# A closing mixture of experts computed in 71 row blocks of each token's two experts, with the decay stage's table products on VectorE

## The reference

```python
# decay attention: phases and decays by position, per head
qph = q * phase_prog;  kph = k * phase_prog_inv
inner = (einsum(qph, kph) * mask) @ v;  cross = (q * phazor_prog * phazor) @ last_conv
t = t + (inner + cross).real
# closing mixture, hidden width 192, top 2 of 8
z = layer_norm(t)
vals, idx = top_k(z @ Wg + bg, 2);  gates = softmax(vals)
h = gelu(einsum('bne,xeh->bnxh', z, W1) + b1)
expert_out = einsum('bnxh,xhe->bnxe', h, W2) + b2
out = t + sum_k gates[k] * expert_out[idx[k]]
```

## Time and profile before

| | us |
|---|---|
| median of three runs | 4375.7 |
| span of the profiled execution | 4435.5 |
| first mixture, blocks (window 2256 to 2630) | 374 |
| decay stage, from its first DMA at 2629.4 to 3681.6 | 1052 |
| closing mixture, from 3681.6 to the end | 754 |

### The profile page before, as it was taken

The page is one execution under the profiler, slowest core; times in us unless marked ns, Lnnn a source line. Parts: engine busy times, 40 slices in busy tenths (PEclk is TensorE's granted clock), DMA queues, the critical chain, the costliest instruction groups (busy, mean ns, idle before and its releaser), DMA issues. The chain is left out here.

```text
span 4435.5 us, 74474 instructions
## 1 busy us (share of the span) xinstructions
PE 3699.2 (83%) x21807; PEld 1993.2 (45%) x21809; DVE 3136.1 (71%) x6481; ACT 2174.3 (49%) x3800; POOL 1933.4 (44%) x2119
## 2 busy tenths in 40 slices
PE   2479999999999999999569962888888886999999
PEld 0212333333333333332258851555555555777777
DVE  7478888888887878887156646555555557877777
ACT  3326666666666666666357740222222223444443
POOL 1111333233223333332345552666666644777776
PEclk9679999999999999999789985999999998999999
DMA  2121111122222222220033320000000001000000
GB/s 97 20 37 28 31 30 30 30 38 38 36 37 38 38 39 38 38 37 11 18 117 103 103 78 10 25 29 28 26 28 28 27 16 34 24 24 24 24 20 23
DMA packets 98451, 166.17 MB, mean 37 GB/s; under 512 B 27904, under 2 KB 33288, under 8 KB 98072
## 3 DMA queue, kind: packets, MB, share of 16 engines
q1 hardware_dynamic: 81208, 129.14, 12.2%
q0 software_dynamic: 16384, 33.59, 2.7%
q10 hardware_dynamic: 576, 0.02, 0.0%
HBM read 89.70 MB, written 72.97 MB: 37 GB/s over the span
## 5 line engine op out<-in xcount | busy, mean ns | idle before, releaser
L1214 ACT ACTIVATE b_probs<-b_ps_s 128x512 f32<-128x512 f32 x2048 | 1174.4, 596 | 673.0 <-PE b_ps_s L1258 609.9
L1016 DVE TENSOR_REDUCE b_maxes<-b_ps_m 128x1 f32<-128x1024 f32 x1024 | 1218.2, 1216 | 312.9 <-PE b_ps_m L1246 288.4
L1258 PE MATMUL b_ps_s<-b_qs,b_ks 99*128 99x512 bf16 x2048 | 790.6, 390 | 83.8 <-DMA b_qs<-b_m_parts 23.4
L1246 PE MATMUL b_ps_m<-b_ks,b_qs 96*128 96x512 bf16 x2048 | 638.5, 394 | 64.2 <-DVE b_maxes L1016 43.5
L1985 POOL TENSOR_TENSOR e_act_lo<-e_act,e_act_hi 128x512 fp32r<-128x512 f32 x384 | 522.6, 1361 | 238.9 <-DVE e_act_hi L1914 238.9
L1258 PEld LDWEIGHTS b_ps_s<-b_qs,b_ks 99*128 99x128 bf16 x2048 | 198.7, 98 | 882.5 <-ACT b_probs L1214 668.2
L1270 PE MATMUL b_ps_o<-b_probs,b_vs 128*32 128x512 f32 x4096 | 551.8, 611 | 23.6 <-ACT b_probs L1214 22.8
L2186 ACT ACTIVATE e_act<-e_ps_h,e_bias 128x512 f32<-128x512 f32 x384 | 264.4, 689 | 411.3 <-PE e_ps_h L2240 290.6
L935 POOL DMA_INDIRECT slots_in<-b_xn,b_slot x256 | 251.6, 983 | 413.2 <-ACT b_probs L1214 367.0
L2089 DVE TENSOR_TENSOR e_act<-e_act,e_ps_g 128x512 f32<-128x512 f32 x384 | 261.6, 682 | 145.7 <-ACT e_act L2186 145.7
L2777 DVE TENSOR_TENSOR d_inner<-d_ps_s,d_decay 128x512 f32<-128x512 f32 x256 | 169.3, 682 | 221.6 <-PE d_ps_s L3059 109.3
(11 more groups left out here) (462 smaller groups left out, 7089.7 us busy)
## 6 DMA issues: line engine op xcount, KB each, us to landing
b_qs<-b_q_parts SPq DMA_DIRECT2D x96, 256.0 KB
c_xin<-slots_in SPq DMA_DIRECT2D x71, 256.0 KB, 2.6
slots_out<-c_y_out SPq DMA_DIRECT2D x71, 256.0 KB, 2.0
b_q_parts<-b_qparts SPq DMA_DIRECT2D x16, 768.0 KB
a_x<-in_x_dram SPq DMA_DIRECT2D x8, 1024.0 KB, 10.2
normalised_t<-d_xT SPq DMA_DIRECT2D x16, 512.0 KB
e_xb<-normalised_t SPq DMA_DIRECT2D x32, 256.0 KB, 2.8
out_dram<-e_total SPq DMA_DIRECT2D x32, 256.0 KB, 2.0
```

The lines of the kernel that those rows point to most:

```text
L1016: nc.vector.tensor_reduce(maxes[:, kv, u:u + 1], ps_m[:, u % 2], AX.X, ALU.max).then_inc(m_free, 1)
L1214: nc.scalar.activation(probs[:, s % PROBS, j * HALF:(j + 1) * HALF], ps_s[:, j % 2], ACT.Exp).then_inc(exp_done, 1)
L1246: last = nc.tensor.matmul(ps_m[:, u % 2, half * HALF:(half + 1) * HALF], qs[0:STACK, buffer, h * PX + qt * P:h * PX + qt * P + P], ks[0:ST ...
L1258: nc.tensor.matmul(ps_s[:, j % 2], ks[0:rows, parity, kv * PX + tt * P:kv * PX + tt * P + P], qs[0:rows, parity, h * PX + half * HALF:h * ...
```

## The change

In the decay stage three things change. The products with the tables move from GpSimd to VectorE, which reads `d_ps_q` in PSUM and adds the bias in the same instruction; ScalarE's copy `d_raw` is gone. For each of a token's two experts a "card" of 130 numbers is laid (the normalised token, its gate weight, its own pair number), a rank among the tokens of the same expert is computed by 9 small matmuls with a triangle of ones, and GpSimd scatters the cards (16 indirect DMAs an image) into `cards_in`. The transposed tokens are no longer stored to DRAM, and the loop over images has two images in its body.

`mixture_stage` is replaced by `cards_stage`, 71 blocks of 512 cards of one expert each (hidden width 192 as 128 + 64), whose result rows are weighed and scattered by GpSimd to the pair's own row in `pair_rows` (4 indirect DMAs a block), and by `closing_stage`, which loads both rows of each token, adds them to the tokens, turns them and writes the output.

```diff
@@ cards_stage: SyncE @@
+            for e in range(E):
+                sp.dma_start(slot_rows(E * REGION + e * SLOTS), xin[:, e]).then_inc(spared, 16)
+            sp.wait_ge(plan, 1)
+            sp.wait_ge(pads_made, 2)
+            for e in range(E):
+                at = sp.value_load(base_i[0:1, e:e + 1], min_val=0, max_val=SLOT_ROWS - SLOTS)
+                sp.dma_start(slot_rows(at), xin[:, e]).then_inc(padded, 16)
+            for e in range(RING_L, E):
+                load_weights(e)
...
+            for j in range(MAX_BLOCKS):
+                load_x(j)
@@ cards_stage: GpSimd @@
+            for j in range(MAX_BLOCKS):
+                pool.wait_ge(x_in[j % RING_X], 16 * (j // RING_X + 1))
+                pool.wait_ge(y_copied, j + 1)
+                for t in range(BT):
+                    nc.gpsimd.indirect_dma_start(
+                        out=pair_rows,
...
+                        in_=y_out[:, j % RING_Y, t], in_offset=None).then_inc(y_sent[j % RING_Y], 16)
@@ cards_stage: VectorE @@
+            for j in range(MAX_BLOCKS):
+                if j + 2 < MAX_BLOCKS:
+                    fetch(j + 2)
+                if j >= 2:
+                    weigh_y(j - 2)
+                if j + 1 < MAX_BLOCKS:
+                    split_x(j + 1)
+                low(j, 0)
+                low(j, 1)
@@ cards_stage: ScalarE @@
+            for j in range(MAX_BLOCKS):
+                first(j, 0)
+                if j >= 1:
+                    add_bias(j - 1)
+                high(j, 0)
+                first(j, 1)
+                if j + 1 < MAX_BLOCKS:
+                    high_x(j + 1)
+                high(j, 1)
@@ cards_stage: TensorE @@
+            for j in range(MAX_BLOCKS):
+                unit(j, 0)
+                if j >= 1:
+                    second(j - 1, 0)
+                    second(j - 1, 1)
+                unit(j, 1)
+                if j + 1 < MAX_BLOCKS:
+                    turn_x(j + 1)
+                if j >= 2:
+                    turn_y(j - 2)
@@ closing_stage: SyncE, VectorE @@
+                for k in range(2):
+                    sp.dma_start(pairs[:, m % RING_P, k],
+                                 pair_rows[k * TOK + m * PX:k * TOK + (m + 1) * PX].rearrange(
+                                     "(p j) c -> p (j c)", j=TILES)).then_inc(pairs_in[m % RING_P], 16)
...
+                nc.vector.tensor_tensor(total[:, m % RING_S], pairs[:, m % RING_P, 0], pairs[:, m % RING_P, 1], ALU.add
+                                        ).then_inc(summed, 1)
+                add_tokens(m)
@@ decay_stage @@
+                if isinstance(n, int) and n == IMAGES:
+                    scatter(n - 1, 1 - parity, 0, 2 * TILES)
...
+            def queries_with_tables(w, g):
+
+                dve.wait_ge(p_ready, 2 * w + 2)
+                for out, table in ((q_chan, tab_k), (q_state, tab_s)):
+                    stt(laid(out[:, g]), laid(ps_q[:]), row[:, g, 3:4], table[:, g:g + 1].broadcast_to([P, CHUNKS, P]),
+                        ALU.add, ALU.mult).then_inc(tables_used, 1)
...
+                    if nxt and c == 0:
+                        keys_with_table(w + 1, (a + 1) % 2)
+                    if nxt and c == 1:
+                        queries_with_tables(w + 1, (a + 1) % 2)
                     if steps and c == 0:
                         masked(w, 0, a % 2)
...
-                positive(pe, p_copied, 2 * w + kind)
+                positive(pe, tables_used, 3 * w + kind)
```

More of the change, by code:

```diff
@@ L1823, in mixture_stage @@
[L1823 to L1832, removed]
@@ L1857, in mixture_stage @@
[L1857 to L1862, removed]
-        def blocks(eng, body):
-            for k in range(2):
-                body(0, k)
-            for k in range(2):
-                body(1, k)
-            with eng.Fori(2, IMAGES - 1) as image:
-                for k in range(2):
-                    body(image, k)
-            for k in range(2):
-                body(IMAGES - 1, k)
@@ L1899, in tail @@
[L1899 to L1914 removed]
+        w_raw = sb("e_w_raw", [P, RING_L, n_w1 + n_w2])
@@ L2121, in _ @@
-            lay_gates(0, 0)
-            make_rows()
-            set_rest(0)
-            assert steps[0] == SET_UP[gated], steps
-            split_x(0, 0)
-            for part in range(3):
-                split_gates(0, 0, part)
-            set_rest(1)
-            dve.wait_ge(bias_ready, 1)
-            blocks(dve, body)
-            if gated:
-                tail(1, weigh)
-            else:
-                tail(HIGH_DELAY, high)
-            if out is None:
-                add_block(IMAGES - 1, 1)
+                count[0] += 1
@@ new lines, in link, with by_block @@
+                ins.then_inc(plan, 1)
+                dve.wait_ge(plan, count[0])
+            def by_block(x):
+                return x.rearrange("p (a e) -> p a e", a=1).broadcast_to([P, MAX_BLOCKS, E])
+            for e in range(E):
+                rows = xin[:, e].rearrange("p t c -> p (t c)")
+                nc.vector.tensor_copy(rows[:, 0:SLOTS], nothing[:])
+                nc.vector.tensor_copy(rows[:, SLOTS:], nothing[:, 0:BT * CARD - SLOTS])
+            dve.wait_ge(const, 3)
+            link(nc.vector.tensor_copy(base_i[:], route["card_base"][:]))
@@ L2263, in turn @@
-            def turn(image, k):
-                pe.wait_ge(y_copied, number(image, k) + 1)
-                for j in range(BT):
-                    last = nc.tensor.transpose(ps_y[:, k, j * P:(j + 1) * P], total[:, k, j * P:(j + 1) * P], ident[:])
-                last.then_inc(y_turned, 1)
-            def body(image, k):
-                first = isinstance(image, int) and image == 0 and k == 0
-                pe.wait_ge(x_lo_done, number(image, k) + 1)
-                for u in range(n_units):
-                    if first and u % set_units == 0:
-                        pe.wait_ge(w_lo_done, u // set_units + 1)
-                    unit(image, k, u)
-                    if gated and u % 2 == 0:
-                        spread_gates(image, k, u // 2)
-                    if not gated:
-                        spread_gates(image, k, u)
-                    late(image, k, u, lag, second)
-                    if u == TURN_AT and out is None and before(image, k):
-                        turn(*before(image, k))
-                    if u == GATES_AT and after(image, k):
-                        turn_gates(*after(image, k))
@@ L2449, in decay_stage @@
         assert sum(GATHERS_AT.values()) == 2 * TILES
+        SCATTERS_AT = {(a, c): 2 - GATHERS_AT.get((a, c), 0) for a in range(4) for c in range(CHUNKS)}
+        assert sum(SCATTERS_AT.values()) == 2 * TILES
         def positive(eng, s, value):
@@ L2629, in body @@
                 for a, c, steps, nxt in slots(n):
+                    if scatters:
+                        first = sum(some for at, some in SCATTERS_AT.items() if at < (a, c))
+                        scatter(n - 2, parity, first, first + SCATTERS_AT[a, c])
                     if a and gathers(n):
```

908 lines of the change are left out of this document (451 added, 457 removed).

## The result

The changed kernel takes 4528.2 us (the median of four runs, 4525.8 to 4534.9) against 4374.9 us before: a ratio of 1.0355, 95% interval 1.034 to 1.037. It is slower, by 153 us, where 110 us less was forecast. Its trace has a span of 4527.1 us, as long as the timed runs.

A forecast was written before the change was run, and what follows sets the result against it. Bounds taken: TensorE's work in the closing mixture, TensorE waiting on VectorE in decay. 3681.6 + 76 + 14 + 1 + 27 + 42 + 382 + 18 + 84 = 4325.6 against 4435.5, so 4266 us timed; wide range 4180 to 4375.

The forecast's parts named there:

- ScalarE then adds the bias, makes the high part and the second gelu before it comes to the next x_hi: Card blocks: ScalarE's three steps, 0.59 + 0.50 + 0.59 = 1.68 us of a 5.35 us chain.
- the ring: Card blocks: chain x_hi, x_lo, nine TensorE products, ScalarE's steps, back to x_hi; 5.35 us, taken as 5.45 a block.
- Rival D: Card blocks: TensorE granted 1.2 GHz, product pitch 0.43, block 7.2 us, 126 us more, 4391 us; chance 0.12.
- The last scatters: End of the decay stage: the last image's 16 card scatters before set-up can begin, 27 us.
- The table products: Decay stage: three products an item added on VectorE, 4.8 us an image, 76 us in 16 images.
- rival B: Decay stage: VectorE's idle time takes the table products whole, 76 us less, 4190 us; chance 0.18.
- The nine rank products: Decay stage: on TensorE's own path, 0.9 us an image, 14 us in all.
- Rival E: Decay stage: card scatters ahead of gathers on GpSimd make VectorE wait 3.75 us an image, 60 us, 4326; chance 0.08.
- Set-up: Start of the cards stage: padding writes, landing and a first block at a low clock, 42 us.
- The drain: End of the card blocks: 10.7 as in the first mixture, 5.1 for four scatters, 2 for landing: 18 us.
- The closing stage: After the cards: 25.2 MB moved, floor 61 us at 412 GB/s, taken as 84 us, range 60 to 110.
- Rival C: Card blocks: VectorE's copy of weights delays GpSimd's scatters, block 5.8 us, 25 us more, 4290; chance 0.15.

The follow-up runs named there:

- two_totals: The changed kernel with two buffers in place of one for the sum with its bias (`e_total`); 4245.1 us, ratio to before 0.9694.
- late_bias: The changed kernel, still one `e_total`, with ScalarE's bias of the previous block moved behind the second gelu and the next x_hi; 4246.5 us, ratio 0.9695.
- early: two_totals with the next block's x turned right behind unit 0 and its high part made ahead of the bias and second gelu; 4238.9 us, ratio 0.9677.
- turn_first: The changed kernel, one `e_total`, with TensorE turning y of block j-2 behind the first unit of block j, ahead of second-layer products; 4332.2 us in one run.
- split_first: early with VectorE making x_lo of the next block ahead of weighing y; 4227.5 us, ratio 0.9663.
- split_act: split_first with the copy of the weights made by ScalarE at the end of its block, not by VectorE; 4224.0 us, ratio 0.9655.

## Why the prediction was wrong

**The blocks.** The step that failed is "ScalarE then adds the bias, makes the high part and the second gelu before it comes to the next x_hi". A block took 9.73 us and not 5.45, 299 us in 70 of them. The order and each duration were right (0.59, 0.51, 0.58 measured for 0.59, 0.50, 0.59), but the bias was given one condition, the second-layer products, and it has two: `act.wait_ge(y_turned, j)` stood in the code. I read how long each step lasts and which product it reads, and did not list, for each buffer with one copy, who must have read it before it is written again. With that wait, TensorE's whole block plus 3.2 us is the ring. two_totals and late_bias show it from two sides. The first mixture's block, which served as the model, gave no warning: it has one buffer `c_total` and the same wait, but ScalarE adds the bias of block j-2 there, not j-1, and stood 3.3 us before it in all 71 blocks together.

**The clock.** Rival D had the pitch of 0.43 right, but as a thing that either comes or not. The busy share was reckoned at 67%; it was 68%, of longer products. Both numbers agree by accident: with the wait gone TensorE is busy 240 of 320 us at a clock of 1.00, and with the wait it stood 3.2 us in a row each block. D's 7.2 us a block was too short, because the low clock stretches a ring that holds all of TensorE's work, not nine products. Had the wait been seen, it would have had to be priced at the low clock too: 7.4 became 9.7. D alone had the kernel slower than before, but for the block that it reckoned with the low clock does not come: with the wait gone it is 1.00. It took the gap of 3.2 us, which D did not have.

**The decay stage.** 99 us longer, 118 forecast, but with the parts wrong. The last scatters cost 31 against 27 forecast. The table products cost 21 to 30 alone, against 76: some two thirds of the term did not come, which is rival B's reason in part (VectorE's idle time takes them). The nine rank products, priced at 0.9 us an image, take about 0.2 us on the timeline of two_totals. The rest, some 38 us, is the cards themselves beside these; which of their instructions it is stays open. And there is a reason for the move that the prediction did not see: without it GpSimd is the bound, and the stage 85 us longer. Rival E put 46 us an image on GpSimd, which does not end an image of 54.6; with the products left there its sum is 61, and it does.

**The ends.** Set-up 37.0 for 42. The drain, 30.4 for 18, holds a last block at the low clock (products 0.43 apart), and its two last blocks' eight scatters came one behind the other. The closing stage took 69.0 for 84: its queues moved 411 GB/s over 50 us [as rows 12], so the floor of 61 was nearly reached, and reads mixed with writes moved as much as reads alone had (412). The Trainium skill puts the limit of such a transfer at about 358 GB/s a core (DMA: Bandwidth & Descriptors, "Where 436 GB/s comes from"); this row is above that, and below the ceiling of some 435 that the same section gives.

**Rival C.** The rule of the Trainium skill (SBUF — State Buffer, "Who interferes with whom") agrees in kind: a scatter that meets the whole of VectorE's two copies (0.61 and 0.15 us) mostly takes 1.7 us in place of 0.96 in the kernel after. That a scatter grows by 0.3 beside the copy of 0.15 alone is more than that copy's length. In the changed kernel none of it should cost time, since GpSimd stands 250 us in 58 blocks for VectorE; no run isolates it.

## What to carry to other kernels

For every buffer that has one copy, write down who reads it last and where that reader stands in its own queue, before summing any durations; a write that waits for the last instruction of a block puts the whole block in series with all that is queued behind the write. Look for a change of order before a second buffer: moving the bias down in ScalarE's list gave 282 us here, as two buffers gave 283. When TensorE has a gap that comes back every block, price it at both clocks, and to learn what the clock alone costs, fill the gap with products that nobody reads.

## What was not expected of the hardware

Filling 3.2 us of TensorE's idle time in each block of 9.7 raised the granted clock from 0.66 to 1.00 and made the kernel 154 us faster, though it does more. With a gap of 1.4 us in 5.7 (two_totals, early) the clock was 1.00 as well; with 1.85 in 6.8 (turn_first) it was 0.87. An indirect DMA's issue on GpSimd, 0.96 us, takes 1.3 us (split_first), 1.6 (two_totals) or 1.7 (kernel after) when VectorE's copies of 896 numbers a partition (0.61 us) and of 3 (0.15 us) fall into it, and about 1.25 when only the copy of 3 does (split_act). Which of VectorE's instructions at that place holds it, the copy or the loading of the expert's number just before, was not isolated.
